# Differential attention: two units of work in one step of TensorE, with another order of the tiles of maxima and of the weight splits

## What is computed

```python
E = 512; H = 16; HD = E // H // 2          # 16 pairs of heads, 16 channels per head
q = (x @ Wq).reshape(b, t, 2 * H, HD).transpose(0, 2, 1, 3) * scaling
k = (x @ Wk).reshape(b, t, 2 * H, HD).transpose(0, 2, 1, 3)
v = (x @ Wv).reshape(b, t, H, 2 * HD).transpose(0, 2, 1, 3)
scores = jnp.einsum('bhqd,bhkd->bhqk', q, k)
causal = jnp.triu(jnp.full((t, t), -jnp.inf, dtype=jnp.float32), 1)
aw = jax.nn.softmax((scores + causal).astype(jnp.float32), axis=-1)
aw = aw.reshape(b, H, 2, t, t)
aw = aw[:, :, 0] - lam * aw[:, :, 1]
attn = jnp.einsum('bhqk,bhkd->bhqd', aw, v)
```

## Time and profile before

| what | value |
|---|---|
| median of three runs | 3913.28 us |
| the profiled execution: time, span | 3907.37 us, 3905.6 us |
| PE busy over the span | 3487.6 us (89%) |
| DVE | 2662.8 us (68%) |
| ACT | 1886.5 us (48%) |
| POOL | 910.8 us (23%) |
| mean granted clock of TensorE | 0.936 of full speed |

### The profile page before, as it was taken

How to read it: one execution, slowest core, us unless ns; L and a number is a source line. 1 busy time by engine, 2 the same in 40 slices (tenths; PEclk the granted TensorE clock), 3 DMA queues, 4 the chain that set the end, 5 groups by cost and what they waited for, 6 DMA issues and landing times. The chain is left out here.

```text
span 3905.6 us, 58521 instructions
## 1 busy us (share of the span) xinstructions
PE 3487.6 (89%) x21032; PEld 2452.6 (63%) x21032; DVE 2662.8 (68%) x5043; ACT 1886.5 (48%) x2413; POOL 910.8 (23%) x823
## 2 busy tenths in 40 slices
PE   8579999999999588964999999999999999819997
PEld 6434444444444377763777777777777777618775
DVE  3177777777775353434899889988998889753333
ACT  3126666666666511222566666666666666422222
POOL 0102222222222100001344434443444344400000
PEclk9769999999999778967999999999999999959998
DMA  7313434343431120035555655565556555450001
GB/s 225 61 33 103 94 100 97 98 96 100 85 97 65 54 81 1 7 131 172 180 177 176 206 183 177 176 208 183 176 176 208 184 177 176 148 210 27 22 0 43
DMA packets 248277, 479.76 MB, mean 123 GB/s; under 512 B 42880, under 2 KB 56448, under 8 KB 243776
## 3 DMA queue, kind: packets, MB, share of 16 engines
q1 hardware_dynamic: 245360, 455.19, 38.2%
q10 hardware_dynamic: 2640, 20.97, 1.3%
HBM read 371.96 MB, written 103.55 MB: 122 GB/s over the span
## 5 line engine op out<-in xcount | busy, mean ns | idle before, releaser
L461 ACT ACTIVATE probs<-prob_scores 128x1024 f32<-128x1024 f32 (+3 forms) x640 | 572.2, 895 | 463.9 <-PE prob_scores L389 456.1
L409 PE MATMUL times_v<-probs,VS 128*64 128x256 f32 (+2 forms) x4608 | 619.5, 385 | 38.0 <-ACT outT L488 36.9
L508 DVE TENSOR_REDUCE part_max<-ring 128x1 f32<-128x512 f32 x768 | 494.0, 686 | 125.6 <-PE ring L381 123.9
L59 PE MATMUL sc_pip<-sc_xh,sc_wl 128*128 128x512 f32 x1024 | 453.6, 443 | 24.8 <-DMA sc_xl<-x_low 20.8
L409 PEld LDWEIGHTS times_v<-probs,VS 128*64 128x64 f32 x4608 | 282.3, 137 | 280.7 <-issue 192.0
L61 PE MATMUL sc_pip<-sc_xh,sc_wh 128*128 128x512 f32 x1024 | 405.8, 396 | 0.0
L60 PE MATMUL sc_pip<-sc_xl,sc_wh 128*128 128x512 f32 x1024 | 402.3, 393 | 0.0
L1383 POOL TENSOR_TENSOR sc_xdd<-sc_xdt,sc_small 128x512 f32<-128x512 f32 x128 | 248.3, 1940 | 640.0 <-DVE sc_xdt L1605 640.0
L381 PE MATMUL ring<-KS,QS 48*128 48x512 f32 (+3 forms) x1280 | 265.2, 410 | 69.8 <-DVE part_max L505 24.7
L389 PE MATMUL prob_scores<-QS,KS 50*128 50x512 f32 (+3 forms) x1280 | 301.8, 468 | 2.2 <-ACT probs L461 2.2
L1596 DVE SCALAR_TENSOR_TENSOR sc_ca<-sc_xr,sc_chan,sc_ca 128x512 f32<-128x512 f32 x384 | 292.5, 762 | 13.6
(11 more groups left out here) (328 smaller groups left out, 6956.7 us busy)
## 6 DMA issues: line engine op xcount, KB each, us to landing
sc_wh<-scan_W_high SPq DMA_DIRECT2D x256, 256.0 KB, 2.7
sc_wl<-scan_W_low SPq DMA_DIRECT2D x256, 256.0 KB, 3.0
sc_ce<-scan_expa SPq DMA_DIRECT2D x128, 512.0 KB, 5.2
sc_woh<-scan_Wo_high SPq DMA_DIRECT2D x128, 256.0 KB, 3.8
sc_wol<-scan_Wo_low SPq DMA_DIRECT2D x128, 256.0 KB, 4.6
w_raw<-in_Wg SPq DMA_DIRECT2D x64, 256.0 KB
scan_W_high<-w_hi SPq DMA_DIRECT2D x64, 256.0 KB, 2.0
scan_W_low<-w_lo SPq DMA_DIRECT2D x64, 256.0 KB, 2.3
```

What stands on the lines that cost most here:

```text
L59: pe.matmul(out, ll, rh, start=start, stop=False)
L409: mm = pe.matmul(po[MV * s:MV * (s + 1), CHUNK - w + n * h:CHUNK - w + (n + 1) * h], VS[p % 2][:, j, :], PT[u % NPT][:, s, n * h:(n + 1) * ...
L461: act.activation(PT[u % NPT][:, :, 0:w], pb[u % 2][:, :, 0:w], ACT.Exp).then_inc(exped, 1)
L508: dve.tensor_reduce(to, slot(n)[:, 0:w], AX.X, ALU.max).then_inc(emptied, 1)
```

## The change

A step now has two units, u and u + 1 with u even. PE does the first unit's tile of maxima, then, each behind its wait for an exponential, the scores of u + 2 and u + 3, then the second unit's tile, then the products with V of u and of u + 1. What stood behind single units (transposed maxima, transposed outputs) stands at the same step. DVE does both tiles of a step, then the rest. `tile_order` lists the tiles anew: the twelve diagonal tiles that are 128, 256 or 384 wide stand at odd numbers, and odd numbers come first in a step (unit u, even, has tile u + 7 or u - 33); the other 28 tiles, all 512 wide, fill the rest in their old order. In steps 2, 6, 14 and 26, which follow a transposed output, the first tile is 512, 256, 128 and 256 wide. The weight splits stand at units 15, 17, 26, 28, 30 and 32 instead of 13, 15, 25, 27, 29 and 31. The number of instructions of each kind stays.

```diff
     units = [(c, j) for c in range(NCH) for j in range(4 * c + 4)]
-    tiles = [(i, c) for i in range(TT) for c in range(i // 4 + 1)]
-    NU, NM = len(units), len(tiles)
+    NU = len(units)
+
+    def tile_order():
+
+        every = [(i, c) for i in range(TT) for c in range(i // 4 + 1)]
+        narrow = [(i, c) for i, c in every if c == i // 4 and i % 4 < 3]
+        wide = [t for t in every if t not in narrow]
+        firsts = [None] * (NU // 2)
+        for n in range(len(narrow)):
+            firsts[n * len(firsts) // len(narrow)] = narrow[n]
+        return [wide.pop(0) if t % 2 == 0 or firsts[t // 2] is None else firsts[t // 2] for t in range(len(every))]
+
+    tiles = tile_order()
+    NM = len(tiles)
...
     for p in range(PAIRS):
-        for u in range(NU):
-            for q, t in step_tiles(p, u):
+        for u in range(0, NU, 2):
+            for q, t in step_tiles(p, u) + step_tiles(p, u + 1):
                 for s in range(2):
                     place["max", q, t, s] = len(place)
...
-    SPLIT_AT = (13, 15, 25, 27, 29, 31)
+    SPLIT_AT = (15, 17, 26, 28, 30, 32)
...
                 for p in range(PAIRS):
-                    for u in range(NU):
-                        n = p * NU + u
+                    for u in range(0, NU, 2):
                         to = p + (u + LEAD) // NU
+                        for q, t in step_tiles(p, u):
+                            max_scores(q, t)
                         if to < PAIRS:
                             if u + LEAD == NU:
                                 pe.wait_ge(max_in[to % NQK], (to // NQK + 1) * 64)
-
-                            pe.wait_ge(exped, n + 1)
-                            scores(to % NQK, (u + LEAD) % NU)
-                        for q, t in step_tiles(p, u):
+                            for v in (u, u + 1):
+
+                                pe.wait_ge(exped, p * NU + v + 1)
+                                scores(to % NQK, (v + LEAD) % NU)
+                        for q, t in step_tiles(p, u + 1):
                             max_scores(q, t)
                         if u == TURN_AT and p + 1 < PAIRS:
                             turn_maxima(p + 1)
                         times_v(p, u)
+                        times_v(p, u + 1)
...
                 for p in range(PAIRS):
-                    for u in range(NU):
-                        for q, t in step_tiles(p, u):
+                    for u in range(0, NU, 2):
+                        for q, t in step_tiles(p, u) + step_tiles(p, u + 1):
                             maxima(q, t)
```

More of the change, by code:

```diff
@@ L199, in attention @@
     EARLY = NU - START
-    assert NU == NM
+    assert NU == NM and NU % 2 == 0 and TURN_AT % 2 == 0 and all(e % 2 for e in ends)
     def step_tiles(p, u):
```

## The result

The changed kernel takes 3934.97 us in the median of six runs (3930.01 to 3939.07), the kernel before 3912.05 us beside it. The ratio is 1.0059, with a 95% interval from 1.0046 to 1.0072: slower by 0.6%, 23 us. The prediction was 3927 us, range 3895 to 3952.

A forecast was written before the change was run, and what follows sets the result against it. PE was taken to bound the loop. Pairs to 974.2 us (+26), late pairs (+1), the end (-14) and small terms (+1) gave +14 on 3907.4, so 3921; with 5.9 for the median, 3927 us, range 3895 to 3952.

The forecast's parts named there:

- What bounds the loop: Attention loop, 320 to 1240 us: PE is the bound, busy 885.5 of 920 us, with 0.40 us of gaps per unit.
- part 1: In the loop, a step of two units pays the 0.40 us mode changes once: -8.0 us per pair.
- Part 2: The second tile's load waits for DVE's reduction, 1.28 us behind a wide tile; with part 1, +2.5 us per pair.
- Part 3: In four steps behind transposed outputs, DVE's combine delays the second tile: +3.4 us per pair.
- Part 4: With splits moved and longer steps, products no longer wait for ACT's copy of the last output: -3.8 us per pair.
- Per pair: Loop time for each pair of heads: +2.4, so 65.97 becomes 68.4 us.
- Part 5: Late pairs from 11 on: +0.8 us over four; the end, where no tiles are left: -14 us.
- the sum: All terms against the profiled run: +26, +1, -14 and +1, so +14 us.
- rival S: One in four new idle times behind the combine lowers PE's clock: +21 us, 3948 us; chance 0.14.
- F: The second tile's weight load is hidden, or DVE's hand-over shorter by as much: -30 us, 3897 us; chance 0.17.
- G: The second tile hardly waits, so part 1 pays in full: 58 us a pair, 3780 us; chance 0.04.
- N: Step terms err by a hundredth or two; drain and wait cancel within 8 us: 3913 us; chance 0.23.

The follow-up runs named there:

- turn_first_short: Changed kernel with output transposes ahead of the step's products and DVE reducing only 64 keys of each tile: 3776.65 us, ratio 0.9665.
- short_maxima_after: Changed kernel with DVE reducing only the first 64 keys of each tile: 3831.47 us, ratio 0.9795.
- turn_first: Changed kernel with the transposes of an output ahead of the step's products instead of behind them: 3888.02 us, ratio 0.9934.
- short_maxima_before: Kernel before with DVE reducing only the first 64 keys of each tile: 3884.13 us, ratio 0.9927.
- new_splits_alone: Kernel before with only the weight splits moved to units 15, 17, 26, 28, 30 and 32: 3884.18 us, ratio 0.9924.
- turn_first_late_splits: Changed kernel with output transposes ahead of the products and weight splits at 16, 18, 28, 30, 32 and 34: 3891.16 us, ratio 0.9959.
- old_split_units: Changed kernel with the weight splits back at units 13, 15, 25, 27, 29 and 31: 3963.92 us, ratio 1.0138.
- old_tile_order: Changed kernel with the tiles of maxima in the order of the kernel before: 3937.95 us, ratio 1.0078.

## Why the prediction was right

**What bounds the loop, and part 1.** Right. The 0.40 us of each change of mode is saved once per step: scores follow scores in 0.2 us, sixteen products take 1.95 us, and turn_first_short, 5.8 us a pair better than one unit in a step, shows most of the gain once the waits are away.

**Part 2, the second tile's wait.** Right to a hundredth: 1.28 us behind a wide tile and 1.10 behind a 384-wide one (1.28 and 1.09), 0.44 on to the products (0.43), 3.59 us for the step (3.58). short_maxima_after shows that this wait is what DVE's reduction costs.

**Part 3, the combine.** Right: 1.63 us between the tiles with a 128-wide first one (1.28 + 0.35), so the combine's delay is 0.75, 0.85, 0.91 and 0.86 us in the four steps, 3.4 in all as forecast. turn_first gives 2.4 us of it back, and between the two kernels with short reductions the same move gives 3.5 (62.97 to 59.5).

**Part 4, copy and splits.** Its amount is nearly right: the waits for the copy went from 36.9 to 0.3 us, and of its 3.8 us a pair 3.1 stay when DVE's reductions are short (short_maxima_before, 65.29 less 62.2 by streams); the other 0.7 were waits for DVE. Its reason is half right. "The splits are out of its way" holds with one unit a step. With two, the copy is hidden to pair 10 with either set of places (behind it the old places cost 1.2 us a pair), and what the places decide is above all whether POOL's subtraction stands beside DVE's combine. The prediction said of POOL only that it keeps its distance of two units. This is the step that looked at too little: POOL's work was checked against SP's queue, not against DVE.

**Per pair.** 68.4 us forecast, 68.60 measured.

**Part 5 and the sum.** The forecast for the profiled run was +14 us, measured +29.2, of which 28.2 to the last copy. By its terms:

- To pair 10 the loss is 35.3 us against 27. Of this 0.2 x 10.9 = 2.2 is the pair's size, and 5.3 are three falls of the clock.
- In the four late pairs it is 5.9 against 0.8. On top of the forecast come 0.8 for the pair's size, 0.6 x 4 for the scaled split at 15, whose subtraction does collide with the combine, and 3.3 for two falls; the last of the four, which runs out of tiles, is 1.3 shorter.
- The end gained 13.0 against 14, but half of it for a reason that the forecast did not have. In new_splits_alone, one unit in a step, the same stretch takes 66.4 us instead of 72.9 (1227.0 to 1293.4), with 3.4 us of it at the lower clock instead of 13.6. So 6.5 of the 13.0 belong to the places of the splits, and the other 6.5 to the step of two units, for which part 5 had at least 8.5. That the sum of the term came out is in part luck.

So the mis-sized term is the clock, which rival S priced at 21 us with one fall in four steps of that kind and the forecast at none: the five falls cost 8.6. The mechanism of S exists and joined the forecast instead of replacing it. S took its odds from the four waits of 1.45 us at unit 12; the four of 1.52 to 1.54 us at unit 24 in the same pairs, of which none was followed by a fall, it left out. In the medians, where the profiled runs' own spread drops out (that of before stood 4.7 us under its median, that of after 1.6 above), the change costs 22.9 us against 14.

**The rivals.** F (the load hidden) and G (no wait) are refuted by 703.82 above. N (within 8 us of before) is refuted by the interval, which starts at +0.46%, 18 us.

## What to carry to other kernels

Before work is put together to save the engine that is the bound a fixed cost, list what now stands closer together than before, and for each pair the buffer that the second needs from the first: here 8.0 us a pair were saved, and more than that was lost in a hand-over of 1.28 us that 1.68 us of other work had hidden. Where such a batch is made, move what the other engine does for somebody else (the combine) behind a long stretch of the bound engine's work: one move of four transposes turned +0.6% into -0.7%. And try the parts of a change alone: the best kernel here has one of its three parts, and that part's gain of 28 us had hidden over half of what the other two cost.

## What the runs showed of the hardware

A subtraction of POOL (128x512, 1.27 us) stops some DVE instructions that run beside it until it ends. A scaling of four elements took 1.32 instead of 0.23 us (held up in 22 of 64 combines of turn_first). A subtraction of 32 elements with both inputs in SBUF took 1.30 instead of 0.19 us (turn_first_late_splits), and the combine's last addition, 128 elements with both inputs in SBUF, 0.95 instead of 0.29 (four times in turn_first). Reductions from PSUM in the same stretches kept their 0.68 us. The Trainium skill, "SBUF — State Buffer", section Who interferes with whom, has the rule: DVE and GpSimd share one pair of ports as an exclusive lock, taken by DVE instructions in a two-port mode or, against a reading GpSimd, with two SBUF inputs. The subtraction, the addition and the reductions agree with it, and so does the size: the wait is the rest of POOL's instruction and has nothing to do with DVE's. Whether the scaling, which has one tensor input, ran in a two-port mode, no view shows. The same section gives the ports to whoever issues first; the recorded starts don't show that, for at 806.99 DVE's scaling starts 0.03 us ahead of POOL's subtraction and is held up all the same.

The clock of TensorE fell to 1.2 GHz for 3.4 us at a time in an otherwise busy loop, at a price of 1.6 to 2.0 us each (pairs of 70.2 and, with two falls, 72.2 us instead of 68.6). The longer the idle time, the more often a fall came soon behind it, at most 2.3 us. Between 320 and 1240 us of before, after, old_split_units and old_tile_order, 3 of 124 idle times of 0.9 to 1.2 us were followed by one, and 16 of 32 from 1.2 to 1.75 us. Idle times of this length are not needed, though: the one fall of turn_first (918.6 us) and the one at 946.6 above had only 0.48 us before them. What tells the cases apart stays open. The runs with few or no long idle times had the fewest falls in this stretch: none in new_splits_alone and one in turn_first, against five after the change and eleven in old_split_units. These are counts of one profiled run each.
